# One stage of 13 groups of four node tiles in place of self loops, graph norm, last layernorm and store

## The reference

```python
deg = segment_sum(ones, dst, n)
loop_attr = segment_sum(edge_attr, dst, n) / jnp.maximum(deg, 1.0)[:, None]
# every node gets one more edge to itself, with loop_attr as its edge attributes
xl, xr, ee = x @ Wl + bl, x @ Wr + br, eattr @ We
msg = xl[src_a] + xr[dst_a] + ee
score = jnp.einsum('ehc,hc->eh', jax.nn.leaky_relu(msg, 0.2), att)
ex = jnp.exp(score - segment_max(score, dst_a)[dst_a])
alpha = ex / (segment_sum(ex, dst_a)[dst_a] + 1e-16)
out = segment_sum(alpha[:, :, None] * xl[src_a], dst_a) + bias_out
o = out - out.mean(axis=0) * gn_mean_scale
out = relu(gn_weight * o / jnp.sqrt((o * o).mean(axis=0) + EPS) + gn_bias)
x = layernorm(x + out)
```

## Time and profile before

| | us |
|---|---|
| median of three runs | 5764.78 (5759.43 to 5767.15) |
| span of the profiled execution | 5760.2 |
| weighted pass, first VectorE op to last | 4857.2 to 5482.9 |
| self loops, to their last VectorE op | 5483.7 to 5588.5 |
| division and graph norm, to the scale | 5605.5 to 5688.1 |
| scaling, residual, last layernorm | 5688.1 to 5744.2 |
| store, to the end | 5744.2 to 5760.2 |

### The profile page before, as it was taken

How to read it: one execution, slowest core, us unless ns; L and a number is a source line. 1 busy time by engine, 2 the same in 40 slices (tenths; PEclk the granted TensorE clock), 3 DMA queues, 4 the chain that set the end, 5 groups by cost and what they waited for, 6 DMA issues and landing times. The chain is left out here.

```text
span 5760.2 us, 89989 instructions
## 1 busy us (share of the span) xinstructions
PE 4064.8 (71%) x18050; PEld 2715.5 (47%) x18051; DVE 3452.3 (60%) x10054; ACT 1431.2 (25%) x3398; POOL 2872.9 (50%) x2883
## 2 busy tenths in 40 slices
PE   0477777776777777748997995989898883555531
PEld 0366666664333333324554653555555552444421
DVE  5788888886556655544332116554444446888846
ACT  0355555553222222210000002222222221000020
POOL 1577777773677777760000001777777770333300
PEclk9865555656676666768998995555555556999955
DMA  5577777775121111117876542666666662555520
GB/s 108 173 248 242 250 252 249 242 249 162 52 61 52 61 52 60 53 28 177 201 167 215 187 145 72 177 176 176 176 174 176 176 163 64 142 142 142 142 72 22
DMA packets 1060959, 846.72 MB, mean 147 GB/s; under 512 B 548416, under 2 KB 954543, under 8 KB 1047349
## 3 DMA queue, kind: packets, MB, share of 16 engines
q1 hardware_dynamic: 788384, 600.79, 34.9%
q0 software_dynamic: 98672, 176.74, 12.0%
q10 hardware_dynamic: 173844, 68.53, 4.9%
HBM read 604.67 MB, written 167.28 MB: 134 GB/s over the span
## 5 line engine op out<-in xcount | busy, mean ns | idle before, releaser
L2130 POOL DMA_INDIRECT ring<-xl_rows,idx x896 | 895.4, 999 | 1283.0 <-DVE idx L2209 1010.1
L1007 POOL DMA_INDIRECT edge_counts<-cntb,placeb x850 | 844.3, 993 | 363.7 <-issue 254.5
L403 POOL DMA_INDIRECT ringa<-x_sign_pos,idxa x880 | 872.3, 991 | 301.6 <-issue 294.9
L2202 PE MATMUL zps<-We,eaT 64*128 64x128 f32 x1792 | 710.8, 498 | 0.0
L2200 PE MATMUL zps<-xr,hotT 128*128 x2688 | 454.3, 301 | 146.8 <-ACT hotT L2182 86.3
L2556 PE MATMUL ops<-val,hot 128*128 128x200 f32 x1792 | 363.6, 346 | 263.5 <-DVE out L2575 138.7
L2202 PEld LDWEIGHTS zps<-We,eaT 64*128 64x128 f32 x1792 | 447.3, 309 | 164.3 <-issue 147.5
L2232 DVE TENSOR_TENSOR z<-zps,ring 128x512 f32<-128x512 f32 x224 | 155.0, 692 | 606.0 <-PE zps L2202 512.2
L488 PE MATMUL sela<-hota,endsa 128*128 128x128 f32 x1760 | 396.7, 396 | 132.0 <-ACT endsa L429 95.9
L2523 POOL TENSOR_TENSOR val<-rows,val 128x512 f32<-128x512 f32 x224 | 235.6, 1052 | 494.4 <-ACT val L2542 494.4
L2556 PEld LDWEIGHTS ops<-val,hot 128*128 128x128 f32 x1792 | 296.0, 190 | 330.9 <-DVE out L2575 205.4
(11 more groups left out here) (348 smaller groups left out, 6345.8 us busy)
## 6 DMA issues: line engine op xcount, KB each, us to landing
edge_counts<-zeroa SPq DMA_DIRECT2D x55, 1568.0 KB
matd<-edge_counts SPq DMA_DIRECT2D x12, 6272.0 KB
keyb<-edge_keys SPq DMA_DIRECT2D x50, 1216.0 KB
dstb<-dst_in_tile SPq DMA_DIRECT2D x112, 512.0 KB
xl_of_steps<-ring SPq DMA_DIRECT2D x224, 256.0 KB
rows<-xl_of_steps SPq DMA_DIRECT2D x224, 256.0 KB
reseta<-resets SPq DMA_DIRECT2D x110, 512.0 KB
dstba<-dst_in_tile_bf ACTq DMA_DIRECT2D x112, 256.0 KB
```

The source lines that it names most:

```text
L403: p.indirect_dma_start(out=ring[:, k, :], out_offset=None, in_=table, in_offset=bass.IndirectOffsetOnAxis(ap=idx[:, k:k + 1], axis=0)).the ...
L1007: p.indirect_dma_start(out=g.M.rearrange("d s -> (d s)").unsqueeze(1), out_offset=bass.IndirectOffsetOnAxis(ap=place[:, i, k:k + 1], axis= ...
L2130: p.indirect_dma_start(out=ring[:, c, k, :], out_offset=None, in_=g.xl_rows[0:N, :], in_offset=bass.IndirectOffsetOnAxis(ap=idx[:, q * GS ...
L2202: ins = t.matmul(zk, eaT[:, c, k, :], g.We[:, :], start=False, stop=True)
```

## The change

`self_loops`, `finish3` and `store` become one block, `node_tail`, that works on 13 groups: twelve of four node tiles (512 columns) and one of two (256 columns). xl and xr are loaded once, with the four vectors, by SP in the weighted pass, behind the row loads of its first turn; their tiles (`g.xl`, `g.xr`, `g.vec`) are allocated before the pass.

In the block, VectorE, POOL, PE, ACT and SP hand groups to each other by semaphores, with two buffers for what passes between them (`lT`, `lk`, `part`, and the PSUM banks `tr` and `zp`). PE transposes straight from `g.out` (no copy `ls`), and VectorE adds its product from PSUM (no copy to `zn`). POOL adds xr and xl, multiplies by att, makes the self-loop term and adds `gn_bias`. The division moves from the rows to the 200 weights. The output bias is not added to the rows: it is put in the vector `shift` that the graph norm subtracts. The sums over the nodes take 512 columns in one matmul, group by group, and VectorE folds the four tiles. ACT squares. In the last part ACT makes the sum of squares of the layernorm with its accumulator, the mean is not subtracted in a pass of its own, and each tile is normalised by one tensor_scalar with mean and root as per-node operands. SP stores each group when it is done.

```diff
@@ -2511,6 +2425,12 @@
                         wait(s, s_val, G - NG + 1)
                         s.dma_start(rows[:, c, :].rearrange("p (k f) -> p k f", k=GS),
                                     g.rows[bass.ds(G * GS, GS), :, :].rearrange("k e f -> e k f")).then_inc(s_r[c], 16)
+                    if isinstance(it, int):
+                        for to, of in ((g.xl, g.xl_rows), (g.xr, g.xr_rows)):
+                            s.dma_start(to[:, :].rearrange("p (t f) -> p t f", f=F), of.rearrange("(t p) f -> p t f", p=P)
+                                        ).then_inc(g.s_early, 16)
+                        for n in g.vec:
+                            s.dma_start(g.vec[n][:, :], a["L3_gnn_" + n].partition_broadcast(P)).then_inc(g.s_early, 16)
                 turns(s, body, TURNS3)
 
             @block.gpsimd
+def node_tail(nc, g, a):
...
+    GT = 4
+    groups = [(lo, min(GT, NTP - lo)) for lo in range(0, NTP, GT)]
+    n = len(groups)
...
+        lT = m.sb("lT", [DE, 2, GT * P])
+        zf = m.sb("zn", [P, NTP * F])
+        lk = m.sb("lkn", [P, 2, GT * F])
+        part = m.sb("partn", [P, 2, GT * F])
...
+                ch.link(v.tensor_scalar(rdeg[:, :], deg, 1.0, None, ALU.max))
+                ch.link(v.reciprocal(rdeg[:, :], rdeg[:, :]))
+                v.tensor_tensor(es, es, bc_last(rdeg[:, :], DE), ALU.mult).then_inc(s_es, 1)
...
+                for i, (lo, w) in enumerate(groups):
+                    v.wait_ge(s_x0, i + 1)
+                    v.wait_ge(s_zp, i + 1)
+                    v.tensor_tensor(flat(zf, lo, w), zp[i % 2][:, 0:w * F], flat(g.xr, lo, w), ALU.add).then_inc(s_z, 1)
+                    v.wait_ge(s_z, i + 1)
+                    wait(v, s_sl, i - 1)
+                    v.scalar_tensor_tensor(out=lk[:, i % 2, 0:w * F], in0=flat(zf, lo, w), scalar=0.2, in1=flat(zf, lo, w),
+                                           op0=ALU.mult, op1=ALU.max).then_inc(s_lk, 1)
+                    if i:
+                        score(i - 1)
+                score(n - 1)
...
+                ch.link(v.tensor_tensor(sl[:, :], sl[:, :], den[:, :], ALU.mult))
+                marks["share"] = ch.n
+                ch.link(v.tensor_tensor(top[:, :], top[:, :], den[:, :], ALU.mult))
+
+                def gathered(i):
+                    lo, w = groups[i]
+                    v.tensor_tensor(flat(zf, lo, w).rearrange("p (t h c) -> p t h c", h=HEADS, c=C),
+                                    acc[:, lo:lo + w, 0:F].rearrange("p t (h c) -> p t h c", c=C),
+                                    heads(top[:, :])[:, lo:lo + w, :].unsqueeze(3).broadcast_to([P, w, HEADS, C]),
+                                    ALU.mult).then_inc(s_t, 1)
+
+                gathered(0)
+                for i, (lo, w) in enumerate(groups):
+                    if i + 1 < n:
+                        gathered(i + 1)
+                    v.wait_ge(s_t, i + 1)
+                    v.wait_ge(s_b, i + 1)
+                    v.tensor_tensor(flat(zf, lo, w), flat(zf, lo, w), part[:, i % 2, 0:w * F], ALU.add).then_inc(s_o, 1)
+
+                def over_tiles(bank):
+                    return bank[:, :].rearrange("p (k f) -> p f k", f=F)
+
+                v.wait_ge(s_mp, 1)
+                ch.link(v.tensor_reduce(total[:, :], over_tiles(mp), AX.X, ALU.add))
+                ch.link(v.scalar_tensor_tensor(out=shift[:, :], in0=total[:, :], scalar=1.0 / N,
+                                               in1=g.vec["bias_out"][:, :], op0=ALU.mult, op1=ALU.add))
+                ch.link(v.tensor_tensor(shift[:, :], shift[:, :], g.vec["gn_mean_scale"][:, :], ALU.mult))
+                ch.link(v.tensor_tensor(shift[:, :], shift[:, :], g.vec["bias_out"][:, :], ALU.subtract))
+                for i, (lo, w) in enumerate(groups):
+                    rows = flat(zf, lo, w).rearrange("p (t f) -> p t f", f=F)
+                    v.wait_ge(s_o, i + 1)
+                    v.tensor_tensor(rows, rows, bc_mid(shift[:, :], w), ALU.subtract).then_inc(s_dev, 1)
...
+                def scaled(i):
+                    lo, w = groups[i]
+                    rows = flat(zf, lo, w).rearrange("p (t f) -> p t f", f=F)
+                    v.wait_ge(s_dev, i + 1)
+                    v.tensor_tensor(rows, rows, bc_mid(scale[:, :], w), ALU.mult).then_inc(s_sc, 1)
+
+                def residual(i):
+                    lo, w = groups[i]
+                    v.wait_ge(s_gb, i + 1)
+                    v.scalar_tensor_tensor(out=flat(g.xflat, lo, w), in0=flat(zf, lo, w), scalar=0.0,
+                                           in1=flat(g.xflat, lo, w), op0=ALU.max, op1=ALU.add).then_inc(s_xr, 1)
+                    v.wait_ge(s_xr, 2 * i + 1)
+                    v.tensor_reduce(neg[:, lo:lo + w], g.x[:, lo:lo + w, :], AX.X, ALU.add).then_inc(s_xr, 1)
+                    v.wait_ge(s_xr, 2 * i + 2)
+                    v.tensor_scalar(neg[:, lo:lo + w], neg[:, lo:lo + w], -1.0 / F, None, ALU.mult).then_inc(s_neg, 1)
+
+                def spread(i):
+                    lo, w = groups[i]
+                    v.wait_ge(s_var, i + 1)
+                    v.tensor_scalar(var[:, lo:lo + w], var[:, lo:lo + w], 1.0 / F, EPS, ALU.mult, ALU.add).then_inc(s_ve, 1)
+
+                def normal(i):
+                    lo, w = groups[i]
+                    v.wait_ge(s_root, i + 1)
+                    v.reciprocal(root[:, lo:lo + w], root[:, lo:lo + w]).then_inc(s_rec, 1)
+                    v.wait_ge(s_rec, i + 1)
+                    for k in range(w):
+                        T = lo + k
+                        ins = v.tensor_scalar(flat(g.xflat, T, 1), flat(g.xflat, T, 1), neg[:, T:T + 1], root[:, T:T + 1],
+                                              ALU.add, ALU.mult)
+                    ins.then_inc(s_fin, 1)
+
+                for i in range(n + 3):
+                    for lag, stage in ((0, scaled), (1, residual), (2, spread), (3, normal)):
+                        if 0 <= i - lag < n:
+                            stage(i - lag)
...
+                for i in range(n - 1):
+                    t.wait_ge(s_o, i + 1)
+                    t.matmul(mp[:, :], g.ones[:, :], flat(zf, *groups[i]), start=i == 0, stop=False)
+                t.wait_ge(s_o, n)
+                t.matmul(mp[:, 0:F], g.valid[:, :], flat(zf, NT - 1, 1), start=False, stop=True).then_inc(s_mp, 1)
+                for i in range(n - 1):
+                    t.wait_ge(s_sq, i + 1)
+                    t.matmul(vp[:, :], g.ones[:, :], part[:, i % 2, :], start=i == 0, stop=False).then_inc(s_vq, 1)
...
+                for i, (lo, w) in enumerate(groups):
+                    e.wait_ge(s_dev, i + 1)
+                    wait(e, s_vq, i - 1)
+                    e.activation(part[:, i % 2, 0:w * F], flat(zf, lo, w), ACT.Square).then_inc(s_sq, 1)
...
+                for i, (lo, w) in enumerate(groups):
+                    e.wait_ge(s_neg, i + 1)
+                    for k in range(w):
+                        T = lo + k
+                        ins = e.activation(part[:, i % 2, k * F:(k + 1) * F], flat(g.xflat, T, 1), ACT.Square,
+                                           bias=neg[:, T:T + 1], accum_out=var[:, T:T + 1])
+                    ins.then_inc(s_var, 1)
+                    if i:
+                        roots(i - 1)
+                roots(n - 1)
...
+            @block.gpsimd
+            def _(p):
+                def sums(i):
+                    lo, w = groups[i]
+                    p.tensor_tensor(flat(g.xr, lo, w), flat(g.xr, lo, w), flat(g.xl, lo, w), ALU.add).then_inc(s_x0, 1)
+
+                p.wait_ge(g.s_early, 16 * 6)
+                sums(0)
+                sums(1)
+                for i, (lo, w) in enumerate(groups):
+                    p.wait_ge(s_lk, i + 1)
+                    at = lk[:, i % 2, 0:w * F].rearrange("p (t f) -> p t f", f=F)
+                    p.tensor_tensor(at, at, bc_mid(g.att[:, :], w), ALU.mult).then_inc(s_at, 1)
+                    if i + 2 < n:
+                        sums(i + 2)
+                p.wait_ge(s_c, marks["share"])
+                for i, (lo, w) in enumerate(groups):
+                    wait(p, s_o, i - 1)
+                    p.tensor_tensor(byhead(part[:, i % 2, 0:w * F]), byhead(flat(g.xl, lo, w)),
+                                    bc_last(sl[:, lo * HEADS:(lo + w) * HEADS], C), ALU.mult).then_inc(s_b, 1)
+                for i, (lo, w) in enumerate(groups):
+                    p.wait_ge(s_sc, i + 1)
+                    rows = flat(zf, lo, w).rearrange("p (t f) -> p t f", f=F)
+                    p.tensor_tensor(rows, rows, bc_mid(g.vec["gn_bias"][:, :], w), ALU.add).then_inc(s_gb, 1)
+
+            @block.sync
+            def _(s):
+                for i, (lo, w) in enumerate(groups):
+                    s.wait_ge(s_fin, i + 1)
+                    if lo + w <= NT - 1:
+                        s.dma_start(out[lo * P:(lo + w) * P, :].rearrange("(t p) f -> p t f", p=P),
```

(10 more changed lines are left out.)

229 lines of the change are left out of this document (80 added, 149 removed).

## The result

The changed kernel takes 5659.9 us (median of four runs, 5656.8 to 5660.3), the kernel before 5764.6 (5759.4 to 5767.2) beside it: a ratio of 0.9818, interval 0.9804 to 0.9832. The span of its profiled execution is 5658.2 us, 102.0 less than before's.

| us | before | after | predicted after |
|---|---|---|---|
| weighted pass: first POOL product to the stage's first VectorE op | 625.6 | 641.1 | 637.6 |
| degrees, division, scores, to the maxima (parts 1 to 3) | 103.6 | 47.5 | 48.2 |
| maxima, exponentials, denominators (4) | | 5.3 | 5.0 |
| weighted sum plus self loop (5) | | 25.7 | 29.5 |
| mean (6) | | 3.1 | 2.4 |

The account below looks back on a forecast made before the run. It took too little overlap, then VectorE's own list of ops, as the bound. The span 5760.2 less 114 for the stage plus 12 for the loads gave 5658, plus 4.6 to the median 5662.5 us; range 5632 to 5695.

Parts of the forecast that it names:

- Part 1: Degrees and edge-sum division at the stage's start: as before to 5488.1, plus 1 us held up by POOL's first sums.
- Part 3: Scores: VectorE and POOL taking turns at 3.0 us a group, PE 3.7 at most; 37.5 us in all.
- Rival (b): PE stays at 1.2 GHz: scores at 3.7 a group (+9), column sums of squares +9; 5681 us, chance 0.15.
- Part 7: Subtraction, squares and their column sums: 1.4 us to fill and 13, PE's first 3.5 us at 1.2 GHz.
- Part 5: Weighted sum plus self loop: VectorE 1.4 plus POOL's turn 0.9, 2.3 us a group; 28.8 and 0.7 to start.
- Part 9: Scaling to normalising: VectorE 4.2 us a group, 52.5 in all, with 1.1 to start and 2.5 to drain.
- Part 10: Store: twelve groups leave while VectorE works, 4.05 us remain behind the last op; end at 5646.2.
- The loads: Loads of xl and xr in the weighted pass make rows 8 14 us late; cost 12 us, between 5 and 20.
- (a): POOL and VectorE hardly disturb each other: scores 2.2, weighted sum 1.4 us a group; 5640 us, chance 0.13.
- (c): Loads in the weighted pass hide, by ACT's lead and the DMA engines' free half; 5650 us, chance 0.08.
- (d): VectorE waits for POOL and ACT in each group from scaling to normalising: 36 us more, 5698 us, chance 0.07.
- (e): Weighted pass falls into a slower step, 3.45 us a group: 162 us more, 5825 us, chance 0.02.

Follow-up runs that it names:

- zeros: The changed kernel with POOL writing zeros in place of the self-loop product in the weighted sum: 5647.6 us, one run.
- product on VectorE: The changed kernel with the self-loop product of the weighted sum made by VectorE instead of POOL: 5654.8 us, one run.
- bf16: The changed kernel with the self loops' product with We made in bf16 on PE: 5648.7 us, one run.

## Why the prediction was right, and where it was off

5662.5 us were predicted and 5659.9 measured. This is closer than its terms, and the closeness is luck: the stage came out 9.6 us shorter than predicted, the pass 3.5 longer, and the scatter ahead of it added 6.1, which sums to nothing (a span of 5658.2 against 5658). The 2.6 us that are left are the step from span to median, 4.6 in the sum and 1.7 here, but for 0.3. What was right beyond luck is the order of the stage, who waits for whom in it, and that the loads hold the pass up by using up SP's lead.

- **What bounds it** (too little overlap first, then VectorE alone) held. With the early loads alone the wait for ScalarE grew by what the load had given back; 56 of the 124 us come from parts 1 to 3, where VectorE sat waiting before.
- **Part 1** 5.8 for 5.4. POOL's first two sums held the division (3.98 for 3.49) as supposed, and also a tiny op on 50 columns, 1.29 us instead of the 0.19 that it takes in the run where POOL's sums wait for the loads at the stage's head.
- **Part 2** first wide op 9.9 us after the start, 9.7 predicted.
- **Part 3** maxima at 47.5 for 48.2, 3.0 a group. (The same point of the kernel before is 5587.3, not 5588.5.) The value was right and half of the reason: I took turn-taking for the pace, but PE set it at 3.0 (1.0 transposes, 2.0 products) up to the eighth group, and the turns only after that. My 3.7 for PE at 1.2 GHz held the fills of two-tile turns, which groups of four don't pay. Rival (b) was right on the clock here and wrong on the price; in part 7 it was wrong on the clock too, which rose.
- **Part 5** 25.7 for 29.5. Here the size was off. The 0.9 for POOL's turn was right (0.86), but VectorE's own 1.4 was the sum of two durations. Ops in a row start 0.60 us apart though each lasts 0.68, so it was 1.2.
- **Part 6** 3.1 for 2.4: matmul and reduction together wait 1.38 us from the last sum on. **Part 8** 2.7 for 2.8.
- **Part 7** 15.8 for 14.4. Here the clock was the term. I let it rise 3.5 us after PE starts. It rose 5.7 us after the first matmul (5588.3), though PE had no gap from that one on (4.70 of the first row's 6 us, which begins 1.3 us earlier):

```profile
5587.00:5593.00 6.00, 4.70 (x6) 1.94 (x7) 6.00 (x11) 2.49 (x4) 0.00 (x0) 0.51 0.00 0
5593.00:5595.00 2.00, 2.00 (x4) 0.78 (x4) 1.54 (x3) 0.72 (x2) 0.00 (x0) 0.75 0.00 0
5595.00:5600.00 5.00, 5.00 (x12) 1.49 (x10) 0.00 (x0) 3.46 (x6) 0.00 (x0) 1.00 0.01 3
```

  In other traces with the same code here it rose 3.4 us after that matmul (loads at the stage's head, zeros) or 5.4 to 5.7 (the change again, product on VectorE), and once it had not fallen at all (bf16). What decides between these the runs don't show, so a forecast of this part can't be closer than 2 to 3 us.

- **Part 9** 47.8 for 56.1, the largest miss, and the same kind as part 5: four tensor_scalars with a row mean of 0.34 take 1.03 together, not 1.40, and the scaling 0.60, not 0.69. That is 0.46 of the 0.55 us a group. "Hardly anything is won here" was wrong by that: 8.3 us were.
- **Part 10** 5.0 for 4.1.
- **The loads** 15.5 for 12, in the range of 5 to 20. The mechanism was right in its first half, rows 8 late by a used-up lead. Two steps were short. SP's two held issues were taken at 9.07 from a stretch without other traffic, and beside the pass's they took 11.07 and 13.03, so group 8 was 16.5 late and not 14. And ACT's running ahead won back only 1.0 of that for VectorE, where I had counted on 2: POOL's last product is 12.8 late, but the 2.7 us more between it and the stage stand in all seven traces with the two whole loads in the first turn (8.9 in six, 11.6 in one), with the pass at 641.0 to 642.4 in each.
- **Rivals.** (a) no turns: false, leaky at 1.1 on average and part 5's sums at 1.42, and 0.68 as soon as POOL doesn't read. (c) loads hidden: false in this place, nearly true when spread. (d) waits on ACT and POOL in part 9: none. (e) the pass out of step: false, 2.76 a group as before.

## What to carry to other kernels

Moving work to GpSimd relieves VectorE only of ops that don't shut it out. Price an op there at what it holds VectorE up, if VectorE has two SBUF operands meanwhile (0.86 us here for 512 columns), against what it would take on VectorE in a row (0.60): give GpSimd what runs beside PSUM reads and reductions, or only writes. And an early load isn't free because the DMA engines have room: put large ones in pieces between the small ones that others wait for, neither ahead of them nor last in a block. When you sum a list of ops on one engine, use the distance between two starts, not the duration.
